# Largest destination score of a graph layer: one GpSimd maximum across partitions in place of two TensorE transposes

## What is computed

```python
Wh = jnp.einsum('bnf,hfd->bhnd', x, W)
ei = jnp.einsum('bhnd,hd->bhn', Wh, a1)
ej = jnp.einsum('bhnd,hd->bhn', Wh, a2)
e = ei[:, :, :, None] + ej[:, :, None, :]
e = jnp.where(e > 0, e, ALPHA * e)
e = jnp.where(adj[None, None] > 0, e, MASK_VAL)
att = jax.nn.softmax(e, axis=-1)
h = jnp.einsum('bhij,bhjd->bhid', att, Wh)
```

## Time and profile before

| | us |
|---|---|
| median of three runs | 2945.73 |
| lowest and highest run | 2943.82, 2947.32 |
| span of the profiled execution | 2943.7 |
| PE busy (27732 matmuls) | 2887.3 |
| DVE busy | 2127.5 |
| ACT busy | 1682.3 |
| POOL busy (917 instructions) | 827.8 |

### The profile page before, as it was taken

The page is one execution under the profiler, slowest core; times in us unless marked ns, Lnnn a source line. Parts: engine busy times, 40 slices in busy tenths (PEclk is TensorE's granted clock), DMA queues, the critical chain, the costliest instruction groups (busy, mean ns, idle before and its releaser), DMA issues.

```text
span 2943.7 us, 68275 instructions
## 1 busy us (share of the span) xinstructions
PE 2887.3 (98%) x27732; PEld 2034.8 (69%) x27732; DVE 2127.5 (72%) x5596; ACT 1682.3 (57%) x3554; POOL 827.8 (28%) x917
## 2 busy tenths in 40 slices
PE   7899999999999999999999999999999999999998
PEld 5566767666767666767667767667767667776766
DVE  5576787776787776877776877776877777877764
ACT  2555655655656655656655656656656656656543
POOL 2123222323222323222233232233222233222221
PEclk9999999999999999999999999999999999999999
DMA  3001011101011101011101011101011111011010
GB/s 102 22 23 45 27 41 45 44 23 45 23 44 45 44 23 44 23 44 44 38 30 44 23 45 44 37 30 44 23 45 44 34 33 40 28 37 37 17 36 30
DMA packets 58840, 109.89 MB, mean 37 GB/s; under 512 B 5568, under 2 KB 41408, under 8 KB 58528
## 3 DMA queue, kind: packets, MB, share of 16 engines
q1 hardware_dynamic: 58032, 104.61, 10.8%
q0 software_dynamic: 496, 0.92, 0.3%
HBM read 88.21 MB, written 17.30 MB: 36 GB/s over the span
## 4 chain that ended last, share of the span: by engine, by line
PE 77%; DVE 12%; POOL 6%; issue 2%; ACT 1%; SPq 0%; DMA 0%; POOLq 0%; DVEq 0%; ACTq 0%
PE ps L972 19%; PE ps L1080 11%; PE ps L1106 8%; PE ps L1115 8%; PE ps L978 8%; PE ps L1142 8%; PE ps L1029 8%; PE ps L958 4%; DVE stats L641 3%; POOL rstd L367 3%; POOL xc L417 3%; DVE pB L753 2%; PE ps L1017 2%; DVE nb L658 1%; DVE hn L829 1%
## 5 line engine op out<-in xcount | busy, mean ns | idle before, releaser
L389 POOL TENSOR_TENSOR qx<-qx,xc 128x512 f32<-128x512 f32 x128 | 163.7, 1279 | 869.4 <-ACT qx L529 869.4
L641 DVE BATCH_NORM_STATS2 stats<-xc 128x6 f32<-128x256 f32 x384 | 134.7, 413 | 328.6 <-POOL xc L399 264.1
L448 ACT ACTIVATE hn<-xc,nb,rstd 128x256 f32<-128x256 f32 x384 | 209.1, 592 | 163.9 <-DVE nb L658 160.7
L1080 PEld LDWEIGHTS ps<-vals,pA 128*64 128x64 f32 x8192 | 253.9, 138 | 54.6 <-issue 54.5
L972 PE MATMUL ps<-wgat,hT 128*128 128x264 f32 x1024 | 267.4, 395 | 1.8 <-ACT hT L457 1.8
L1080 PE MATMUL ps<-vals,pA 128*64 128x65 f32 x8192 | 266.4, 223 | 2.1 <-DVE pA L753 2.0
L1080 PE MATMUL ps<-vals,pB 128*64 128x65 f32 x8192 | 264.0, 223 | 0.3 <-DVE pB L753 0.2
L1080 PEld LDWEIGHTS ps<-vals,pB 128*64 128x64 f32 x8192 | 249.7, 138 | 16.8 <-issue 16.7
L457 ACT COPY hT<-ps 128x1024 f32<-128x1024 f32 x128 | 129.7, 1013 | 224.0 <-PE ps L958 219.8
L1106 PE MATMUL ps<-qx,qT 64*128 64x512 f32 x1024 | 249.8, 614 | 1.1 <-DVE hn L767 0.8
L364 POOL TENSOR_SCALAR rstd<-mv 128x4 f32<-128x4 f32 x160 | 75.0, 469 | 610.2 <-DVE mv L650 610.2
(11 more groups left out here) (147 smaller groups left out, 6194.3 us busy)
## 6 DMA issues: line engine op xcount, KB each, us to landing
qT<-r_dram SPq DMA_DIRECT2D x64, 512.0 KB, 3.9
hT<-r_dram SPq DMA_DIRECT2D x64, 512.0 KB, 4.9
x_in<-in_x SPq DMA_DIRECT2D x32, 512.0 KB, 3.9
out_x<-xc SPq DMA_DIRECT2D x32, 512.0 KB, 3.0
pX<-in_adj SPq DMA_DIRECT2D x1, 1024.0 KB, 8.1
r_dram<-growT SPq DMA_DIRECT2D x64, 8.0 KB, 1.3
pX<-in_L_gnn_W SPq DMA_DIRECT2D x2, 256.0 KB, 5.2
pA<-in_L_gnn_a POOLq DMA_DIRECT2D x8, 64.0 KB, 8.8
```

What stands on the lines that cost most here:

```text
L641: last = nc.vector.bn_stats(stats[s][:, t, :], src[:, t, :])
L1080: last = nc.tensor.matmul(ps[lo:hi, BANK[f"G{g}.{h}"], t * DV:(t + 1) * DV], gat_p[s][h % 2][:, j, t * P + lo:t * P + hi], vals[s][:, j, h ...
```

## The change

For both layers the two transposes on PE and the second maximum on DVE go. POOL gets one instruction instead, `partition_all_reduce` with the maximum, which reads `dm` (128x4) and writes to `dtop` (128x4) the maximum over all partitions, in every partition. `gat_shift` reads `dtop` in SBUF where it read PSUM. In POOL's order `gat_top(c, 3)` stands behind `plus_beta(b)` and ahead of `residual0(a, 0)`, and `gat_top(a, 1)` stands behind `deviation(a, 1)` and ahead of `gat_residual(c, 3, 0)`. PE keeps a wait for `qx` where the first transpose stood.

```diff
+            def gat_top(w, g):
+                if w is None:
+                    return
+                dm_ready[g].wait(pool, w)
+                nc.gpsimd.partition_all_reduce(dtop[w.s][:, :], dm[w.s][:, :], P, REDUCE.max).then_inc(
+                    dtop_ready[g].sem, 1)
...
-                deviation(c, 3); gat_residual(b, 1, 1); deviation(b, 2); plus_beta(b); residual0(a, 0)
-                residual0(a, 1); gat_values(c, 3); deviation(a, 1); gat_residual(c, 3, 0)
+                deviation(c, 3); gat_residual(b, 1, 1); deviation(b, 2); plus_beta(b); gat_top(c, 3)
+                residual0(a, 0); residual0(a, 1); gat_values(c, 3); deviation(a, 1); gat_top(a, 1); gat_residual(c, 3, 0)
...
-            def gat_max(w, g):
-                if w is None:
-                    return
-                dT_ready[g].wait(dve, w)
-                nc.vector.reduce_max(dmax[w.s][:, :], ps[0:H, BANK[f"d{g}"], 0:P], AX.X).then_inc(dmax_ready[g].sem, 1)
-
...
-                top = ps[:, BANK[f"bc{g}"], 0:H].unsqueeze(1).broadcast_to([P, NT, H])
-                dmax_bc[g].wait(dve, w)
+                top = dtop[s][:, :].unsqueeze(1).broadcast_to([P, NT, H])
+                dtop_ready[g].wait(dve, w)
...
-            def gat_max_across(w, g):
-                if w is None:
-                    return
-                dm_ready[g].wait(pe, w)
-                nc.tensor.transpose(ps[0:H, BANK[f"d{g}"], 0:P], dm[w.s][:, :], ident[:, :]).then_inc(dT_ready[g].sem, 1)
-
-            def gat_max_spread(w, g):
-                if w is None:
-                    return
-                dmax_ready[g].wait_apart(pe, w, 1)
-                nc.tensor.transpose(ps[:, BANK[f"bc{g}"], 0:H], dmax[w.s][:, 0:1].broadcast_to([H, P]),
-                                    ident[0:H, 0:H]).then_inc(dmax_bc[g].sem, 1)
...
-                qx_ready[3].wait(pe, c, 1); aggregate0(a, 0); gat_max_across(c, 3); transposed(b, 2, 1)
-                weights_transposed0(a, 2); weights_transposed0(a, 3); gat_max_spread(c, 3)
+                qx_ready[3].wait(pe, c, 1); aggregate0(a, 0); qx_ready[3].wait(pe, c, 2); transposed(b, 2, 1)
+                weights_transposed0(a, 2); weights_transposed0(a, 3)
...
-                gat_aggregate(c, 3, 1); gat_max_across(a, 1)
+                gat_aggregate(c, 3, 1); qx_ready[1].wait(pe, a, 2)
```

More of the change, by code:

```diff
@@ L16, in gnn_stack_kernel @@
     AX = mybir.AxisListType
+    REDUCE = bass.bass_isa.ReduceOp
     P = 128
@@ L79, in gnn_stack_kernel @@
         dm = sets("dm", [P, H])
-        dmax = sets("dmax", [H, 1])
+        dtop = sets("dtop", [P, H])
         gexp = sets("gexp", [P, 2, NT, H])
@@ L205, in gnn_stack_kernel @@
         dm_ready = per_gat("dm_ready")
-        dT_ready = per_gat("dT_ready")
-        dmax_ready = per_gat("dmax_ready")
-        dmax_bc = per_gat("dmax_bc")
+        dtop_ready = per_gat("dtop_ready")
         gexp_ready = per_gat("gexp_ready", 3)
@@ L431, in first @@
                 pool.wait_ge(ident_ok, 3)
-                deviation(a, 0); load_biases(); residual0(a, 0); residual0(a, 1); deviation(a, 1)
+                deviation(a, 0); load_biases(); residual0(a, 0); residual0(a, 1); deviation(a, 1); gat_top(a, 1)
                 pool.wait_ge(bias_in, BIASES)
@@ L851, in slot @@
                 softmax_shift0(a); statistics(b, 2); lrelu0(a, 1); mean_and_variance(b, 2); lrelu0(a, 2)
-                shift_of_norm(b, 2); lrelu0(a, 3); second_vectors(a); weights_out0(a, 1); gat_max_t(c, 3); gat_max(c, 3)
+                shift_of_norm(b, 2); lrelu0(a, 3); second_vectors(a); weights_out0(a, 1); gat_max_t(c, 3)
                 inverse_sum0(a); gat_shift(c, 3); weights_out0(a, 3); gat_rows_out(c, 3); statistics(a, 1)
@@ L863, in slot @@
                 masked_max2(b, 1, 3, 1); gat_max_t(a, 1); softmax_shift2(b, 1); gat_weights(c, 3, 2, 3)
-                gat_norm(c, 3, 1); gat_max(a, 1); weights_out2(b, 1, 0); inverse_sums2(b, 0)
+                gat_norm(c, 3, 1); weights_out2(b, 1, 0); inverse_sums2(b, 0)
                 weights_out2(b, 0, 1); gat_shift(a, 1); gat_weights(c, 3, 3, 0, 1, 2); gat_rows_out(a, 1)
@@ L943, in first @@
                 mean_and_variance(a, 1); shift_of_norm(a, 1); poison(); adjacency_out(); gat_max_t(a, 1)
-                gat_max(a, 1); gat_shift(a, 1); gat_rows_out(a, 1)
+                gat_shift(a, 1); gat_rows_out(a, 1)
                 dve.wait_ge(setup_ok, SETUP)
@@ L1209, in slot @@
                     idle_turns(BANK["G3.1"], 8)
-                gat_aggregate(c, 3, 1); gat_max_across(a, 1)
+                gat_aggregate(c, 3, 1); qx_ready[1].wait(pe, a, 2)
                 weights_transposed2(b, 1, 0)
                 masked2[1].wait(pe, b, 8); weights_transposed2(b, 1, 1); weights_transposed2(b, 0, 1)
-                gat_max_spread(a, 1); weights_transposed2(b, 1, 2)
+                weights_transposed2(b, 1, 2)
                 pT2_dve[1].wait(pe, b, 1); weights_transposed2(b, 0, 2); weights_transposed2(b, 1, 3)
@@ L1278, in first @@
                 idle_turns(6, 4); q_rows(a, 1, 0); q_rows(a, 1, 1); q_rows(a, 1, 2); q_rows(a, 1, 3)
-                qx_ready[1].wait(pe, a, 1); pe.wait_ge(setup_ok, 6); gat_max_across(a, 1)
-                gat_max_spread(a, 1); gexp_ready[1].wait(pe, a, 2); pe.wait_ge(setup_ok, 5); gat_rows(a, 1)
+                qx_ready[1].wait(pe, a, 1); pe.wait_ge(setup_ok, 6); qx_ready[1].wait(pe, a, 2)
+                gexp_ready[1].wait(pe, a, 2); pe.wait_ge(setup_ok, 5); gat_rows(a, 1)
                 pe.wait_ge(setup_ok, SETUP)
```

## The result

| | before | after |
|---|---|---|
| median of the runs, us | 2945.97 | 3255.51 |
| lowest to highest run | 2943.82 to 2947.32 | 3253.26 to 3256.95 |
| ratio to before, 95% interval | | 1.1053, 1.1037 to 1.1069 |
| span of the profiled execution | 2943.7 | 3252.4 |
| of that, with TensorE at half clock | 17.8 | 315.7 |

The kernel became 10.5% slower: 3255.5 us where 3300 was forecast, within the range of 3190 to 3500. A slot costs 9.75 us more (98.36 against 88.61; the 88.7 given ahead is 0.1 too long); 31 of them are 302 us of the 308.7 between the two spans.

The account below looks back on a forecast made before the run. PE, busy 98%, was taken as the bound, so any pause adds time. A slot: 1.7 + 6.5 + 1.2 + 2.3 - 0.45 = 11.25 us; 31 slots 349, ends 5, on 2943.7 plus 2.0: 3300 us, range 3190 to 3500.

Parts of the forecast that it names:

- The place: Reload exposed in layer 3 of graph c behind `plus_beta(b)`, 31 slots; in layer 1 hidden in POOL's idle time.
- The pause: PE waits ahead of layer 3's `gat_rows` for POOL's maximum: 1.7 us + reload + maximum, 9.4 us a slot.
- the constant 1.7: Part of layer 3's pause besides reload and maximum, with the maximum standing behind `plus_beta(b)`: 1.7 us.
- the 128 KB row: Profile row behind the reload term, POOL's library change ahead of layer 3's maximum: 6.5 us.
- the power's row: Profile row of POOL's power of 128x4, 1.20 us, used as the time of the maximum.
- the rival built on that: Reload paid only when the waiting instruction is released, so layer 1 pays too: 18.6 us a slot, 3535 us; chance 0.08.
- The clock: PE at half clock behind each layer 3 pause, losing half of 3.4 to 6.8 us: 2.3 us a slot.
- The gain: PE's removed transposes, 0.60 us a slot; 0.15 in layer 3 written off as lost to waiting, 0.45 gained.
- The reload back: POOL's return to library 0 behind layer 3's maximum: hidden ahead of `residual0(a, 0)` unless it takes over 7.4 us.
- The ends: Reload back delays values in graph 0's opening, 1.5 us, and in the last slot, 3.2 us: 5 us.
- A free reload: Rival: reload costs 0.25 us, leaving a 3.2 us pause, 4.4 us a slot, 3082 us; chance 0.08.
- The faster case: Maximum overtakes the wait and runs beside `plus_beta`; PE never pauses, 0.6 us a slot back, 2927 us; chance 0.01.

Follow-up runs that it names:

- The runs by layer: The kernel before with the maximum on GpSimd in one layer only: layer 3 alone, ratio 1.1095; layer 1 alone, ratio 0.9979.
- the run with the copy: The kernel after with a plain 128x4 copy on GpSimd in place of each maximum, so without its reloads: 2980.85 us, ratio 1.0121.
- the run with 34 products: The kernel after with 34 unread products on TensorE ahead of layer 3's `gat_rows` in each steady slot: 3182.83 us, ratio 1.0806.
- The unread maximum: The kernel before with layer 3's maximum added on GpSimd behind `plus_beta(b)`, its result read by nobody: 3228.26 us, ratio 1.0968.

## Why the prediction was right

**The place.** As forecast, the pause is in layer 3 of graph c, behind `plus_beta(b)`, 31 times, ended by ScalarE's `grow`, and layer 1 is hidden. The runs by layer show it: 1.1095 and 0.9979.

**The pause.** Forecast 9.4 us, measured 7.97: (251.4 - 2 x 2.2 of the two ends) / 31. Its terms: the constant 1.7 (1.6 in the run with the copy, whose pause of 1.80 has a step of 0.19 in it), the reload 5.87 instead of 6.5, the maximum 0.39 instead of 1.2. No run shows that a reload is a transfer: the 6.5 of the sum is the 128 KB row, and the pages have the same DMA traffic with 129 reloads as with one (109.88 MB against 109.89, HBM read 88.21 MB in both). That it came within 0.63 us is luck. Nor does any run show how GpSimd makes a maximum across partitions: the 1.2 of the sum is the power's row, and the 0.39 measured lies near the copy's 0.21; over the copy's 0.19 in the same place it is 0.2 us more.

The reload is not put off until the wait is released: the maximum of layer 1 starts 0.14 us after `dm`. So the rival built on that, 3535 us, is wrong.

**The clock.** Forecast 2.3 us a slot, measured 2.3 by the run with 34 products. The size was right by luck, for its working was not: the fall lasts 10.24 us in 23 of the 31 slots (6.83 in seven, 13.65 in the last) and not 3.4 to 6.8, but it begins inside the pause, 3.55 us into it in the slot shown. Only 5.87 us of work lie in it there, and 4.86 on average over the 31. Half of that is 2.4, close to what the run gives back. (The kernel before has a fourth stretch of half clock that the forecast did not name, from 2939.48 to its end; TensorE does nothing in it.)

**The gain.** Forecast 0.45 us. What is left over of the slot, 9.75 = 7.97 + 2.32 - gain, gives 0.54, and the run with the copy 0.55: most of the 0.15 that was written off comes back too.

**The reload back.** It takes 6.7 to 7.6 us where it can be seen, and not 6.5, which is about the whole cover of 7.4 that the forecast found. That nothing came of it has a reason the forecast had only touched ("what the clock adds"): `residual0` starts 9.43 us behind `gat_rows` (1585.17 against 1575.74) where it was 6.53 before, since the work between runs at the fallen clock. How near it was is shown by the run with 34 products, which has the full clock there: `residual0` starts 7.28 us behind the maximum in most slots and still waits for ScalarE's `hn`, not for the reload, so the cover was just enough. The unread maximum shows what the reload costs without a pause ahead of it.

**The ends.** Forecast 5 us, and 308.7 - 302.4 leaves 6.3. That this is near was luck, for the parts were too low: graph 0's `gat_rows` comes 1.6 us later, where no delay was forecast; from there to the next slot's it is 78.4 us after (61.67 to 140.03) and 73.7 before (60.11 to 133.77), 4.7 against the 1.5 forecast; behind the last `gat_rows` 28.5 against 24.0 us, 4.5 against 3.2. That is 10.8 us. What makes up for it: the first slot with a pause is 7.2 us longer than before (96.09 against 88.87) where a steady one is 9.75, the last one 8.9, and the stretch ahead of the last `gat_rows` is 1.0 us shorter.

**The rivals.** A free reload (3082 us) is excluded by the 5.85 us. The faster case hung on the maximum overtaking `plus_beta`, which it does in none of the 31 slots, though `dm` is ready at 1563.99 in the one shown, 2.43 us before `plus_beta` starts; put ahead of it by hand, it took away the pause and 294 us, so a pause does depend on that order. Its 2927 us were not reached: of the 0.6 us a slot, the gap of 0.7 that the reload back makes leaves nothing, and the ends cost 10 us.

In sum, a slot was forecast at 11.25 us and is 9.75. The difference is the reload (0.63) and the maximum (0.81), both taken too high, and the gain, taken 0.1 too low. In 31 slots it makes 46 us; the distance from 3300 to 3255.5 is 44.5, since the ends and the time outside the span were taken some 2 us too low together.

## What to carry to other kernels

In these kernels a maximum across partitions among GpSimd's elementwise steps cost two reloads, a median of 5.9 us there and 7.1 to 7.3 back. Whoever adds one should look for idle time of GpSimd on both sides, not just ahead of the result's reader, and look at the first and last passes of a loop by themselves: here they had less of it, and cost 10 us even where the steady slots gained. Look for that time as the gap between two steps of its own queue, and put the instruction at the gap's start. A VectorE operation on 128x4 took 1.23 us here instead of 0.16 beside a GpSimd operation on 128x512, and keeping the two apart was worth 0.51 us a slot: on a critical chain, look at the highest duration of its line, not at the mean.

## What was not expected

- The reload back was longer than the one there: with a median of 7.1 to 7.3 us (6.7 to 7.9) against 5.9 (5.6 to 6.5), over the kernels that show both.
- In layer 1 the reload ran while the maximum behind it waited for `dm`: 0.14 us from `dm` to the maximum, after 17.85 us of idle time.
- The maximum over 128 partitions of four columns takes 0.39 us in 34 places and 0.88 in the 30 of steady layer 1. The waiting does not make it longer: for graph 0 it waits 9.71 us and takes 0.39. In all 30 places VectorE has started a step on 128x512 0.11 us ahead of it (below, for the slot shown), and in none of the 34. The copy in its place takes 0.19 us in layer 3 and 0.7 to 0.8 in layer 1, beside the same step. So it looks as if the two engines delay each other in both directions; no run was made for this one.

```profile
1609.65 0.75 DVE L753 SCALAR_TENSOR_TENSOR pA<-hT,gval,adjT 128x512 f32<-128x512 f32 x1
```

- The pauses of 8 us brought mostly 10.24 us of half clock (23 of 31 slots), which in 28 of 31 began 2.1 to 3.8 us into the pause; the pauses of 1.8 us in the steady slots of the run with the copy brought none (10.9 us in the whole run).
- `nb`, VectorE's operation on 128x4, goes from 0.16 to 1.23 us beside a GpSimd operation of 1.26 us. The kernel before had this in 30 places, and taking it away was worth more than the change to GpSimd was in its best form.
